# A Mamba-2 block with adaLN: the differences of the decays computed on ScalarE, not on VectorE

## The reference

```python
cs = jnp.cumsum(x, axis=-1)                      # x = dt * A, never positive
diff = cs[..., :, None] - cs[..., None, :]
mask = jnp.tril(jnp.ones((l, l), dtype=bool))
return jnp.exp(jnp.where(mask, diff, 0.0)) * mask   # L
...
Y_diag = jnp.einsum('bcln,bcsn,bhcls,bcshp->bclhp', Cb, Bb, L, Xb)
states = jnp.einsum('bcln,bhcl,bclhp->bchpn', Bb, decay_states, Xb)
Y_off = jnp.einsum('bcln,bchpn,bhcl->bclhp', Cb, states, state_decay_out)
```

## Time and profile before

| what | us |
|---|---|
| median of three runs (1736.09 to 1740.42) | 1739.21 |
| span of the profiled execution | 1740.9 |
| TensorE busy | 1569.5 |
| VectorE busy | 1248.8 |
| ScalarE busy | 627.0 |
| GpSimd busy | 492.0 |

### The profile page before, as it was taken

How to read it: one execution, slowest core, us unless ns; L and a number is a source line. 1 busy time by engine, 2 the same in 40 slices (tenths; PEclk the granted TensorE clock), 3 DMA queues, 4 the chain that set the end, 5 groups by cost and what they waited for, 6 DMA issues and landing times. The chain is left out here.

```text
span 1740.9 us, 26906 instructions
## 1 busy us (share of the span) xinstructions
PE 1569.5 (90%) x8289; PEld 1276.2 (73%) x8289; DVE 1248.8 (72%) x2460; ACT 627.0 (36%) x1208; POOL 492.0 (28%) x440
## 2 busy tenths in 40 slices
PE   5989889988988898989988999875899999999998
PEld 5977777767767777767777777753688888888887
DVE  3779998888888988988988889853546445544543
ACT  3345445444554454434544444430211111201200
POOL 1323423433334233433342333433011111111111
PEclk9799999998999999989998999986899999999999
DMA  8312212121121111211221121104320120120110
GB/s 259 126 42 76 98 46 74 68 79 73 61 84 67 42 73 67 79 73 37 87 83 49 73 67 67 74 31 144 146 73 7 67 73 12 60 72 18 54 49 26
DMA packets 61377, 124.25 MB, mean 71 GB/s; under 512 B 13296, under 2 KB 15984, under 8 KB 56816
## 3 DMA queue, kind: packets, MB, share of 16 engines
q1 hardware_dynamic: 55632, 114.68, 18.9%
q10 hardware_dynamic: 5664, 8.65, 1.4%
HBM read 97.62 MB, written 25.69 MB: 71 GB/s over the span
## 5 line engine op out<-in xcount | busy, mean ns | idle before, releaser
L819 DVE SCALAR_TENSOR_TENSOR xBC<-conv_in,wconv,xBC 128x256 f32<-128x256 f32 x480 | 300.0, 629 | 12.7 <-ACT xBC L616 1.3
L1398 ACT ACTIVATE silu_gate<-bank,sgate 128x512 f32<-128x512 f32 x88 | 60.7, 689 | 383.4 <-PE bank L1517 383.4
L1183 PE MATMUL bank<-X,B_rows 128*128 128x512 f32 x128 | 90.8, 799 | 92.9 <-DVE state L955 88.7
L1452 DVE SCALAR_TENSOR_TENSOR hidden<-bank,sup,silu_gate 128x512 f32<-128x512 f32 x88 | 66.0, 750 | 145.8 <-PE bank L1517 145.8
L615 ACT ACTIVATE conv_in<-bank 128x256 f32<-128x256 f32 x160 | 61.5, 385 | 255.6 <-PE bank L1086 255.6
L1171 PEld LDWEIGHTS bank<-X,decay 128*128 128x128 f32 x1024 | 123.6, 195 | 30.8 <-issue 23.7
L1517 PE MATMUL bank<-ff_h_high,W_gate 128*128 128x512 f32 x352 | 141.5, 402 | 2.4 <-DVE ff_h_low L1440 2.4
L1171 PE MATMUL bank<-X,decay 128*128 128x64 f32 x1024 | 127.0, 278 | 16.4 <-DVE X_D L948 16.4
L1517 PE MATMUL bank<-ff_h_low,W_gate 128*128 128x512 f32 x352 | 140.1, 398 | 0.0
L1549 PE MATMUL bank<-W_down,hidden_high 128*128 128x512 f32 x352 | 139.5, 396 | 0.0
L1549 PE MATMUL bank<-W_down,hidden_low 128*128 128x512 f32 x352 | 139.5, 396 | 0.0
(11 more groups left out here) (170 smaller groups left out, 3493.2 us busy)
## 6 DMA issues: line engine op xcount, KB each, us to landing
decay<-sums_scratch SPq DMA_DIRECT2D x32, 1024.0 KB, 4.7
wq_rows<-wqT SPq DMA_DIRECT2D x33, 256.0 KB, 4.0
widened_scratch<-wq_rows SPq DMA_DIRECT2D x33, 256.0 KB, 2.0
x_tile<-x SPq DMA_DIRECT2D x32, 256.0 KB, 2.8
x_resid<-x SPq DMA_DIRECT2D x32, 256.0 KB, 2.7
x_scratch<-x_resid SPq DMA_DIRECT2D x32, 256.0 KB, 2.0
ff_x_tile<-x_scratch SPq DMA_DIRECT2D x32, 256.0 KB, 3.6
ff_x_resid<-x_scratch SPq DMA_DIRECT2D x32, 256.0 KB, 4.0
```

Source lines behind the costliest of these rows:

```text
L819: nc.vector.scalar_tensor_tensor(A.xc[b][:, m, :], A.raw[:, m, j:j + SC], A.wconv[:, m, j:j + 1], A.xc[b][:, m, :], ALU.mult, ALU.add).the ...
L1183: nc.tensor.matmul(state[:, 0:W], A.Btok[:], A.X[:, f * W:(f + 1) * W], start=True, stop=True).then_inc(state_done, 1)
L1398: nc.scalar.activation(B.sg[m % 2][:], gates[m % 2][:], ACT.Silu, scale=T.sgate[:, m:m + 1]) \
L1452: nc.vector.scalar_tensor_tensor(B.hid[m % 2][:], ups[m % 2][:], T.sup[:, m:m + 1], B.sg[m % 2][:], ALU.mult, ALU.mult).then_inc(hid_step, 1)
```

## The change

The 32 VectorE instructions go. ScalarE computes relu(column - x) in 32 instructions of the same shape, in place, with the column as bias and -1 as scale; that is the negative of min(x - column, 0). Its exponentials then take a scale of -1. The first 16 (c = 0) stand behind `evac_ln`, ahead of `widen`; the other 16 behind `exp_sums`. The semaphore `diff_done` (four a turn) becomes `fall_done` (two a turn).

```diff
+            def falls(u, c):
+
+                wait(act, cs_in[c], u, 16, 16)
+                wait(act, sums_step, u, 3, 3)
+                for h in range(H):
+                    x = A.L[c][:, h, :]
+                    last = nc.scalar.activation(x, x, ACT.Relu, bias=A.s3[:, c * H + h:c * H + h + 1], scale=-1.0)
+                last.then_inc(fall_done, 1)
+
             def exp_decay(u, c, f):
-                wait(act, diff_done, u, 2 * NC, 2 * c + f + 1)
+                wait(act, fall_done, u, NC, c + 1)
                 x = A.L[c][:, f * HH:(f + 1) * HH, :]
-                nc.scalar.activation(x, x, ACT.Exp).then_inc(decay_done, 1)
+                nc.scalar.activation(x, x, ACT.Exp, scale=-1.0).then_inc(decay_done, 1)
...
                 if own:
+                    falls(n, 0)
                     widen(n, 1)
                     silu_tile(n, b, 8)
                     silu_tile(n, b, 9)
                     exp_sums(n)
+                    falls(n, 1)
                     exp_decay(n, 0, 0)
...
-                wait(dve, diff_done, n, 2 * NC, 0)
+                wait(dve, fall_done, n, NC, 0)
                 nc.vector.tensor_copy(A.s3[:, 0:2 * NC * H], small[:, 0:2 * NC * H]).then_inc(sums_step, 1)
...
-            def diff(u, c, f):
-
-                if f == 0:
-
-                    wait(dve, cs_in[c], u, 16, 16)
-                    wait(dve, sums_step, u, 3, 3)
-                for h in range(f * HH, (f + 1) * HH):
-                    last = nc.vector.tensor_scalar(A.L[c][:, h, :], A.L[c][:, h, :], A.s3[:, c * H + h:c * H + h + 1],
-                                                   0.0, ALU.subtract, ALU.min)
-                last.then_inc(diff_done, 1)
...
-                if own:
-                    diff(n, 0, 0)
-                    diff(n, 0, 1)
-                    diff(n, 1, 0)
-                    diff(n, 1, 1)
```

More of the change, by code:

```diff
@@ L356, in mixer_stage @@
             sem(s) for s in ("stats_step", "normed", "split", "conv_step", "softplus_step", "sums_step"))
-        tail_step, diff_done, G_masked, M_done, Xdec_done = (
-            sem(s) for s in ("tail_step", "diff_done", "G_masked", "M_done", "Xdec_done"))
+        tail_step, fall_done, G_masked, M_done, Xdec_done = (
+            sem(s) for s in ("tail_step", "fall_done", "G_masked", "M_done", "Xdec_done"))
         yoff_read, ydiag_read, S_step = sem("yoff_read"), sem("ydiag_read"), sem("S_step")
```

## The result

| | us |
|---|---|
| before, median of 4 runs | 1737.65 |
| changed, median of 4 runs | 1860.13 |
| ratio | 1.070 (95%: 1.067 to 1.073) |
| span of the profiled execution, before and after | 1740.9 and 1858.1 |

The forecast was 1878. The mixer carries all of the loss: its last residual (L567) is done at 1199.7 us before and at 1317.5 now, and some 541 us follow in both.

The account below looks back on a forecast made before the run. VectorE and TensorE were taken to trade the lead, with ScalarE's queue full at the boundary. Delays of 10 x 9.2 + 5 x 7.9 + 7.2 = 139 us on 1740.9 gave 1880, 1878 as median; range 1815 to 1925.

Parts of the forecast that it names:

- The removal is covered: At the turn's end, TensorE's output product hides VectorE's 6.36 us of subtractions; removing them gains 0.1 us.
- 0.30 us a Relu, two table loads a turn: On ScalarE, 32 added Relus at 0.30 us make 9.6 us a turn, with table loads still two a turn.
- Rivals 1 and 3: Relus: another table than silu and exp, 1919 or 1960, chance 0.06; or no overlap, 0.40 us each, 1929, chance 0.10.
- Silus later by 4.8, exponentials by 9.6, the bank by 8.6: Delays at the boundary behind ScalarE's Relus; the second z/dt tile waits for the output product's bank, stalling TensorE 7 us.
- 1.4 us absorbed by VectorE's lateness: VectorE already read the first y_diag 1.4 us late, so that reading comes 8.6 - 1.4 = 7.2 us later.
- Clock 2.0 us: TensorE runs at a lower clock behind its new stall, adding 2.0 us (1.4 to 2.9) up to y_diag.
- Sum at a boundary: Delay per turn boundary: 9.2 us at ten, 7.9 at five back edges, 7.2 at the sixteenth.
- Nothing later gives it back: After the first y_diag reading VectorE works without a wait, so the 9.2 us delay goes into the turn whole.
- Rival 2: Cheaper Relus (1832), or TensorE's next state-bank wait swallowing 2.8 us of each delay (1836); chance 0.16 for either.
- Rival 4: VectorE bounds the whole turn, so removing its 6.36 us a turn gives 102 us less, 1637; chance of faster 0.03.
- The signs: Expected profile: VectorE idle 12 to 15 us a boundary, clock 0.5 behind TensorE's stall, state-bank waits and feed-forward part unchanged.

Follow-up runs that it names:

- e1: The kernel before without its 32 subtractions a turn and without the Relus: 1723.6 us, 0.994.
- e2: The changed kernel with VectorE's 32 subtractions a turn put back beside the Relus: 1857.7 us, 1.070 against the kernel before.
- e5: The changed kernel with the output product's evacuation (c = 1) moved ahead of exp_sums, the second Relus and the exponentials: 1831.9 us, 1.056 against the kernel before.
- e6: The changed kernel with 58 dummy transposes on TensorE in its stall before the second z/dt tile: 1836.8 us, 1.059 against the kernel before.
- e3: The changed kernel with Relus for c = 0 only, the c = 1 subtractions back on VectorE: 1783.5 us, 1.027 against the kernel before.
- e9: The kernel before with the first state reading ahead of conv(1) and two normalisations moved behind conv(9), subtractions still on VectorE: 1695.6 us, 0.978.

## Why the prediction was right, and where it was off

The direction, the mechanism and most sizes held, and the time was 18 us too high. Two sizes were off in opposite directions and hid each other (4 and 5), and one step failed (7).

1. *The removal is covered.* Right in kind (e1, e2). Taken as 0.1 us a turn, it is 11 us in all (e1).
2. *0.30 us a Relu, two table loads a turn.* Measured 0.298, mean 393 ns. Rivals 1 and 3 fell with the groups.
3. *Silus later by 4.8, exponentials by 9.6, the bank by 8.6.* The output's evacuation came 17.67 - 8.35 = 9.3 us later relative to the layer norm, and the wait for the bank was 6.6 us for 7.0. Right in these sizes. But the path was drawn through the bank alone, and e5 shows that it is one gate of two: with the bank freed early only 28 of the 122 us come back, since ScalarE's evacuation of x also follows the exponentials.
4. *1.4 us absorbed by VectorE's lateness.* Too much. In e6, at the full clock, the boundary is 7.3 us longer than before, where the sum without its clock term gives (10 x 7.2 + 5 x 5.9) / 15 = 6.8. e3 shows the same (3.07 us left of 4.8, where I had 2.4).
5. *Clock 2.0 us.* Measured 1.8 on TensorE's stretch, but only 1.24 of it reached VectorE's reading (e6). VectorE is 1.0 us late there at the full clock and just in time at the slow one, so items 4 and 5 overlap: one is 0.5 too low and the other 0.8 too high. That their sum came out is luck in part.
6. *Sum at a boundary.* (10 x 9.2 + 5 x 7.9) / 15 is 8.8 a boundary, measured 8.57.
7. *"Nothing later gives it back".* This step failed. 1.8 us a turn, 15 x 1.8 = 27 us, came back, 1.18 of the 1.8 between the second states product and the copy of the sums and 0.45 in the last stretch. I had added the clock's loss at the boundary and kept all the losses that were already there. In the changed kernel each of these two stretches runs at the full clock in every second turn, and in e6, which takes the slow stretch at the boundary away, the first of the two is slow in every turn again and the last in none. With that the sum is 139 - 27 = 112, for 117 in the profiled spans; the first turns, which the mean leaves out, grew by more.
8. *Rival 2* named a place for the giving back, TensorE's wait for the state bank. That wait did not shrink (88.7 to 86.5); only what follows it did. *Rival 4* (VectorE bounds the turn) fell with e1.
9. *The signs.* VectorE stands still for 17 us at the boundary, where I had 12 to 15. The clock behind the stall is 0.75 in the mean, not 0.5. The later waits for the state bank stayed, and the feed-forward part is as long as it was.

What stays open: why the slow stretches sit where they do from turn to turn. The rows give their places and not their rule, and I did not try to steer them one by one.

## What to carry to other kernels

An engine that is busy for 48% of a stage has no room where its queue is full. Before moving work to it, read its timeline at the very place where the work must stand, and ask who waits for the instructions behind it: here 9.55 us on an engine with half its time free cost 7 us a turn, and the same instructions in its gaps left the time where it had been. A gap is often another engine's wait, and closes when that wait is mended; so mend the wait first, and then see whether there is still anything to move. And of two engines that trade the lead, the one whose load is taken off gains little (here 11 us of 102) if the load stood under another's cover.

## What the runs showed of the hardware

Two normalisations on VectorE took 4.62 us where they met GpSimd's work on y (559.73 in the timeline of the kernel before, with GpSimd's addition from 558.69 for 3.37 and its product from 562.22 for 1.85), and 1.00 us where they met nothing, in e9:

```profile
613.34 1.00 DVE L797 TENSOR_SCALAR x_tile<-x_tile,mean_var,rstd 128x512 f32<-128x512 f32 x2
```

The convolution that came into their place then took 5.48 us for three instructions and not 1.5. But all convolutions together grew by only 11.8 us, while the normalisations fell by 50.7, so the move gets rid of most of this price. I had not seen it in the groups: their mean of one, 2123 ns, mixes 28 instructions of 2.06 to 2.62 us and 4 of 0.54 to 0.55; in e9 all 32 take 0.54 to 0.55.

Relus following one another overlap: 393 ns each from start to end, 298 apart. A stall of 6.7 us on TensorE was followed by 7.8 us at a mean granted clock of 0.75, between the two levels of 1.2 and 2.4 GHz; 58 transposes of nothing in the same stall kept it at 1.00.
